# An AdaLN block of attention scan and FP4 feed-forward: the mix is turned by DMA as 16-bit planes, and the next group's work stands earlier in each engine's order

## What is computed

```python
h = _layernorm(x, axis=-1) * (1 + ca) + sa
x = x + ga * _L0_attn_ref(h, ...)      # RMS norm; q, kv, a = h @ W.T; a = sigmoid(a)
                                       # y[t] = a[t] * y[t-1] + kv[t];  returns q * y
h = _layernorm(x, axis=-1) * (1 + cb) + sb
x = x + gb * _L0_ffn_ref(h, ...)       # fp4_linear gate, up; silu(gate) * up; fp4_linear down
```

## Time and profile before

| | |
|---|---|
| median of 3 runs | 1963.17 us (1962.25 to 1963.4) |
| the profiled execution | 1961.58 us, of which the span of the trace is 1959.8 |
| mean granted TensorE clock | 0.998 |
| PE, DVE, ACT, POOL busy | 99%, 86%, 32%, 61% |
| DMA queue of SP | 45.1% of 16 engines' span |

### The profile page before, as it was taken

One profiled execution on the slowest core, in us unless ns is written; L12 is line 12 of the kernel. 1 busy time (PEld: TensorE's weight loads), 2 busy tenths in 40 slices (PEclk: granted clock), 3 DMA queues, 4 the chain that ended last, 5 costly groups with the idle time before them and its releaser, 6 DMA issues.

```text
span 1959.8 us, 27185 instructions
## 1 busy us (share of the span) xinstructions
PE 1936.3 (99%) x9403; PEld 927.2 (47%) x9403; DVE 1686.6 (86%) x2106; ACT 629.5 (32%) x885; POOL 1198.9 (61%) x1072
## 2 busy tenths in 40 slices
PE   8999999999999999999999999999999999999998
PEld 3444444444444444444444444444444444444444
DVE  7786767676868999999999999999999999999986
ACT  4333433343413233233233323323232332322221
POOL 1554764546535777677667667767766776776641
PEclk9999999999999999999999999999999999999999
DMA  8866665757552433433433343343334334333323
GB/s 292 272 178 144 174 170 149 174 142 200 125 129 69 108 74 80 98 75 72 92 89 72 81 100 74 74 94 88 73 84 96 72 76 97 80 72 87 88 62 77
DMA packets 421251, 218.22 MB, mean 111 GB/s; under 512 B 359858, under 2 KB 359870, under 8 KB 421188
## 3 DMA queue, kind: packets, MB, share of 16 engines
q1 hardware_dynamic: 421188, 217.39, 45.1%
HBM read 95.43 MB, written 33.57 MB: 66 GB/s over the span
## 4 chain that ended last, share of the span: by engine, by line
PE 87%; DVE 6%; issue 2%; POOL 2%; DMA 1%; ACT 1%; SPq 1%; DVEq 0%; POOLq 0%
PE bank L1067 43%; PE bank L986 20%; PE bank L1087 15%; PE bank L1091 7%; PE bank L1011 1%; SPq L398 1%; DVE arena L1163 1%; DMA arena<-arena 1%; DVE bn L1152 1%; DVE arena L1292 0%; DMA arena<-in_L_attn_x_dram 0%; DVE arena L1454 0%; PE bank L925 0%; DMA arena<-in_L_ffn_w_up_dram 0%; DVE arena L1461 0%
## 5 line engine op out<-in xcount | busy, mean ns | idle before, releaser
L1067 PE MATMUL bank<-wgu_hi,arena 128*128 128x512 f16 (+1 forms) x3072 | 869.9, 362 | 2.0 <-DVE arena L1401 2.0
L1067 PE MATMUL bank<-wgu_lo,arena 128*128 128x512 f16 (+1 forms) x1536 | 555.7, 362 | 0.0
L986 PE MATMUL bank<-arena,wq_hi 128*128 128x512 f16 x1536 | 458.5, 380 | 2.3 <-DMA arena<-arena 1.3
L1067 PEld LDWEIGHTS bank<-wgu_hi,arena 128*128 128x128 f16 x3072 | 300.5, 98 | 310.1 <-issue 2.4
L986 PE MATMUL bank<-arena,wq_lo 128*128 128x512 f16 x768 | 292.3, 381 | 0.0
L1087 PE MATMUL bank<-wd_hi,arena 128*128 128x512 f16 x693 | 263.0, 379 | 0.1
L1087 PE MATMUL bank<-wd_lo,arena 128*128 128x512 f16 x693 | 263.0, 380 | 0.0
L986 PEld LDWEIGHTS bank<-arena,wq_hi 128*128 128x128 f16 x1536 | 150.0, 98 | 178.4 <-issue 3.7
L1067 PEld LDWEIGHTS bank<-wgu_lo,arena 128*128 128x128 f16 x1536 | 150.2, 98 | 153.7
L663 POOL TENSOR_TENSOR arena<-arena 128x512 f32<-128x512 f32 x63 | 153.2, 2431 | 95.4 <-DVE arena L1476 95.4
L1401 DVE SCALAR_TENSOR_TENSOR arena<-bank,small,arena 128x512 f32<-128x512 f32 (+1 forms) x192 | 134.1, 701 | 85.8 <-PE bank L1067 81.5
(11 more groups left out here) (162 smaller groups left out, 2743.6 us busy)
## 6 DMA issues: line engine op xcount, KB each, us to landing
arena<-in_L_attn_x_dram SPq DMA_DIRECT2D x32, 1024.0 KB, 5.9
arena<-x_scratch SPq DMA_DIRECT2D x128, 256.0 KB, 3.2
x_scratch<-arena SPq DMA_DIRECT2D x16, 1024.0 KB, 4.4
out_dram<-arena SPq DMA_DIRECT2D x64, 256.0 KB, 3.1
arena<-in_L_wmod_dram SPq DMA_DIRECT2D x6, 1024.0 KB, 14.4
arena<-arena SPq DMA_TRANSPOSE x258, 3.5
wgu_hi<-in_L_ffn_w_gate_dram SPq DMA_DIRECT2D x1, 2816.0 KB, 12.3
wgu_lo<-in_L_ffn_w_up_dram SPq DMA_DIRECT2D x1, 2816.0 KB, 19.0
```

Of the source, the lines that this page charges most:

```text
L986: last = pe.matmul(dst[m % 2][:, :].rearrange("p (j t) -> p j t", j=NJ), w[:, k, at], uT[p][:, half, :, k, :], start=(n == 0), stop=(n == ...
L1067: last = pe.matmul(dst[n][:, 0:w], xT[p][:, half, k, :], wt[:, k, cut], start=(m == 0), stop=(m == 3 * KD - 1))
```

## The change

The 256 transposes of TensorE go, and with them `mixT`, `mix_turned` and TensorE's waits for them. In their place:

- `mix` writes its product over the decay buffer. It keeps the last column of each state in `carry` (a copy of 128x1), so two state buffers serve instead of four.
- `split_mix` (ScalarE, 4 in a group, 128x1024 16-bit elements): copies the float32 product as two planes of 16-bit words, low and high, into `mix_bits`. `decays` of the chunk two later waits for it.
- `turn_mix` (SP, 2 in a group): one transposing DMA for chunks 0 and 1, one for 2 and 3, each 2048 16-bit columns (16 blocks of 128).
- `join_mix` (ScalarE, 4 in a group, 128x1024 16-bit elements): puts the planes together again into one of two row buffers, from which `add_x` reads instead of from PSUM.

The order of work changes on four engines. In group i, ScalarE now does all `squares` and, behind the first two joins, `u_hi` ahead of the second chunk's decay; `apply(i + 2)` stands before the last decay. VectorE does the statistics and `u_lo` ahead of the second chunk's `mix`. SP turns the next u ahead of storing x1. In group 15 the second-half turn of group 14, the storing and the first-half turn of group 15 all stand ahead of `turn_x(0)`. The `add_x` of group 15 moves from the start of tile 0 to its end.

```diff
+        mix_bits = view(CH * GT).bitcast(U16).rearrange("p (q h j m t) -> p q h j m t", q=2, h=2, j=NJ, m=HC)
...
+        mixT_bits = view(NJ * D).bitcast(U16).rearrange("p (q h j c) -> p q h j c", q=2, h=2, j=NJ)
...
+        state = [view(GT) for _ in range(2)]
+        mix_rows = [view(D) for _ in range(2)]
...
+                def turn_mix(i, q):
+
+                    sp.wait_ge(mix_split, CH * i + HC * (q + 1))
+                    wait(sp, mix_joined, NJ * i)
+                    sp.nop(nofuse=True)
+                    sp.dma_start(mixT_bits[:, q].rearrange("p h j (m c) -> p (h j m) c", c=P),
+                                 mix_bits[:, q].rearrange("p h j m t -> p (h j m t)"),
+                                 transpose=True).then_inc(mixT_loaded[q], 16)
...
+                    if i:
+                        turn_mix(i - 1, 1)
+                    if i == NGA - 1:
                         for t in range(2):
                             load_normalised(t + 2, t)
+                    if i < NGA - 1:
+                        turn_u(i + 1, 1 - p)
                     weight_turns(i, -1, 0)
                     if i == 0:
-                        turn_u(1, 1)
                         load_group(3)
                         ffn_rows()
                         load_weights(0)
+                        turn_mix(0, 0)
                     else:
                         sp.wait_ge(x1_ready, NJ * i)
                         sp.dma_start(x1_group[i - 1], xr).then_inc(x1_stored, 16)
+                        turn_mix(i, 0)
+                        if i < NGA - 1:
+                            load_group(i + 3)
                         sp.wait_ge(x1_stored, 16 * i)
                     sp.dma_start(xr, x_group[i]).then_inc(xr_loaded, 16)
-                    if 0 < i < NGA - 1:
-                        turn_u(i + 1, 1 - p)
-                        load_group(i + 3)
                     weight_turns(i, 1, 3)
...
-                sp.wait_ge(x1_ready, NJ * NGA)
-                sp.dma_start(x1_group[NGA - 1], xr).then_inc(x1_stored, 16)
-                sp.wait_ge(x1_stored, 16 * NGA)
+                turn_mix(NGA - 1, 1)
                 for t in range(-1, 3):
                     slot(t, t % 2)
+                    if t == 0:
+                        sp.wait_ge(x1_ready, NJ * NGA)
+                        sp.dma_start(x1_group[NGA - 1], xr).then_inc(x1_stored, 16)
+                sp.wait_ge(x1_stored, 16 * NGA)
...
-                    wait(act, state_ready, CH * i + m - 1)
...
+                def split_mix(i, m):
+
+                    q = m // HC
+                    act.wait_ge(mix_ready, CH * i + m + 1)
+                    wait(act, mixT_loaded[q], 16 * i)
+                    act.activation(mix_bits[:, q, :, :, m % HC, :],
+                                   decay[m % 2].bitcast(U16).rearrange("p (j t h) -> p h j t", j=NJ, h=2),
+                                   ACT.Copy).then_inc(mix_split, 1)
+
+                def join_mix(i, js):
+
+                    for q in range(2):
+                        act.wait_ge(mixT_loaded[q], 16 * (i + 1))
+                    for j in js:
+                        wait(act, x1_ready, NJ * i + j - 1)
+                        act.activation(mix_rows[j % 2].bitcast(U16).rearrange("p (q c h) -> p q c h", q=2, h=2),
+                                       mixT_bits[:, :, :, j, :].rearrange("p q h c -> p q c h"),
+                                       ACT.Copy).then_inc(mix_joined, 1)
...
+                    split_mix(i - 1, 3)
                     decays(i, 0)
                     if not more:
-
+                        join_mix(i - 1, (0, 1))
                         ffn_apply(0, 0)
                         ffn_apply(1, 1)
-                    weights(0)
-                    if more:
-                        squares(i + 1, 1 - p, (0, 1))
-                    decays(i, 1)
-                    if more:
-                        squares(i + 1, 1 - p, (2, 3))
-                        u_hi(i + 1, 1 - p)
-                    else:
+                        decays(i, 1)
+                        split_mix(i, 0)
+                        weights(0)
+                        join_mix(i - 1, (2, 3))
                         steps_of_x(0, 0)
                         x_hi(0, 0)
+                        weights(1)
+                        decays(i, 2)
+                        split_mix(i, 1)
+                        weights(2)
+                        ffn_apply(2, 0)
+                        steps_of_x(1, 1)
+                        decays(i, 3)
+                        split_mix(i, 2)
+                        x_hi(1, 1)
+                        ffn_apply(3, 1)
+                        weights(3)
+                        return
+                    squares(i + 1, 1 - p)
+                    join_mix(i - 1, (0, 1))
+                    u_hi(i + 1, 1 - p)
+                    decays(i, 1)
+                    split_mix(i, 0)
+                    weights(0)
+                    join_mix(i - 1, (2, 3))
                     weights(1)
                     decays(i, 2)
-                    weights(2)
-                    if not more:
-                        ffn_apply(2, 0)
-                        steps_of_x(1, 1)
-                    decays(i, 3)
                     if i + 2 < NGA:
                         apply(i + 2, p)
-                    if not more:
-                        x_hi(1, 1)
-                        ffn_apply(3, 1)
+                    split_mix(i, 1)
+                    weights(2)
+                    decays(i, 3)
+                    split_mix(i, 2)
                     weights(3)
                 groups(group)
+                split_mix(NGA - 1, 3)
...
-                def turn_mix(i, p, js):
-                    for j in js:
-                        if j == 0:
-                            pe.wait_ge(mix_ready, CH * (i + 1))
-                        wait(pe, x1_ready, NJ * i + j - 1)
-                        for m in range(CH):
-                            last = pe.transpose(t_bank[j % 2][:, m * P:(m + 1) * P], mixT[p][:, m, j * P:(j + 1) * P],
-                                                ident[:, :])
-                        last.then_inc(mix_turned, 1)
...
-                    if i == 1:
-                        pe.wait_ge(mod_copied, NROW)
-                    turn_mix(i - 1, 1 - p, (0, 1))
                     product_a(i, p, 1)
                     product_kv(i, p, 1)
-                    turn_mix(i - 1, 1 - p, (2, 3))
...
-                        turn_mix(NGA - 1, 1, (0, 1))
+                        pe.wait_ge(mix_ready, CH * NGA)
                     if not (isinstance(i, int) and (i < 2 or i == LAST)):
                         down(i - 2, p)
                     gate_up(i, p, 1)
-                    if isinstance(i, int) and i == 0:
-                        turn_mix(NGA - 1, 1, (2, 3))
...
-                    dve.tensor_tensor_scan(state[m], decay[m % 2], kv_bank[m % 2][:, :],
-                                           0.0 if first else state[m][:, GT - 1:GT],
+                    if not first:
+                        dve.wait_ge(carry_ready, CH * (i - 1) + m + 1)
+                    dve.tensor_tensor_scan(state[m % 2], decay[m % 2], kv_bank[m % 2][:, :],
+                                           0.0 if first else carry[:, m:m + 1],
                                            ALU.mult, ALU.add).then_inc(state_ready, 1)
                     dve.wait_ge(state_ready, CH * i + m + 1)
+                    dve.tensor_copy(carry[:, m:m + 1], state[m % 2][:, GT - 1:GT]).then_inc(carry_ready, 1)
                     dve.wait_ge(q_ready, CH * i + m + 1)
-                    wait(dve, mix_turned, NJ * (i - 1))
-                    dve.scalar_tensor_tensor(mixT[p][:, m, :], q_bank[m % 2][:, :], ga[:, m, b:b + 1], state[m],
+                    dve.scalar_tensor_tensor(decay[m % 2], q_bank[m % 2][:, :], ga[:, m, b:b + 1], state[m % 2],
...
-                        dve.wait_ge(mix_turned, NJ * i + j + 1)
-                        dve.tensor_tensor(xr[:, j, :], t_bank[j % 2][:, :], xr[:, j, :], ALU.add).then_inc(x1_ready, 1)
+                        dve.wait_ge(mix_joined, NJ * i + j + 1)
+                        dve.tensor_tensor(xr[:, j, :], mix_rows[j % 2], xr[:, j, :], ALU.add).then_inc(x1_ready, 1)
...
+                        add_x(i - 1, (2, 3))
+                        mix(i, p, b, 1, first)
+                        quantise_x(0, 0)
+                        first_stats(2)
+                        x_lo(0, 0)
+                        weights(1)
+                        mix(i, p, b, 2, first)
+                        weights(2)
+                        quantise_x(1, 1)
+                        mix(i, p, b, 3, first)
+                        x_lo(1, 1)
+                        first_stats(3)
+                        weights(3)
+                        return
+                    if two_more:
+                        stats_mean_var(i + 2, p)
                     add_x(i - 1, (0, 1))
```

(26 more changed lines are left out.)

31 lines of the change are left out of this document (21 added, 10 removed).

## The result

| | before | after |
|---|---|---|
| median of the runs, us | 1963.3 (1962.3 to 1964.1, 4 runs) | 2040.1 (2039.1 to 2041.5, 4 runs) |
| profiled execution, span | 1959.8 | 2037.4 |
| ratio of after to before | | 1.0392, interval 1.0374 to 1.0410 |

The change costs 77 us. I had said 1945, with a range of 1933 to 1967. A group of the middle takes 34.7 to 34.9 us, which is the group time of rival 3's milder case (34.7), but its price, the 16 blocks as such, is not what makes it.

A forecast was written before the change was run, and what follows sets the result against it. TensorE, busy 99% of the span, was taken to bound the kernel. 1961.6 - 24.4 - 3 + 1.5 + 7.7 + 1.7 - 1 = 1944.1, plus 1.6 to the median: 1945.7, say 1945 us, range 1933 to 1967.

The forecast's parts named there:

- rival 3: SP and DMA engines: the two 16-block turns make the ring longer than the old group; slower, chance 0.17.
- rival 3's milder case: SP: half of the 16-block turns' extra pro-rata issue time gives 34.7 us a group, 1992 us in all.
- Removed, 24.4 us: TensorE, groups 1 to 14: 16 transposes fewer save 1.74 us a group, if each can run in 31.08 us.
- ScalarE's copies, 1.0: ScalarE: each split or join copy takes 1.0 us, bounds 0.7 and 2.1; ScalarE busy 21.7 of 31 us.
- SyncE: 1.5 issue, 4.5 landing: SP and DMA engines: each 16-block transposing DMA takes 1.5 us to issue and 4.5 to the landing.
- The ring, 30.4 to 32.4: Second-half landing through joins, add_x, store and SP's burst to the next landing: 30.4 to 32.4 us against 31.08; cost 1.5.
- Store to landing: The ring's part on SP, from the store of x1 to the next second-half landing: 19 to 21 us.
- from the landing to the store of x1: The ring's part through the joins and VectorE's work to the last add_x: 11.4 us.
- Early hitches, 3 us taken back: First stage: 8.3 us go in early hitches, of which 3 us (0 to 7) would come back.
- Hand-over, +7.7 and +1.7 of clock: Last group to tile 0: turned x lands later, +7.7 us; TensorE idles some 7 us, its slowed clock adds 1.7.

The follow-up runs named there:

- e14: The changed kernel with the weights' load early, their turns late, and SyncE's turns and loads spread in groups 1 to 14: 1988.8 us, ratio 1.013.
- h2: The kernel before, with groups 6 to 13 by DMA, weights' load early, their turns late, SyncE's DMAs spread: 1947.6 us, ratio 0.992.
- e12: The kernel before with only 4 of TensorE's 16 transposes a group left from group 1 on (stale data): 1957.2 us, ratio 0.997.
- e7: The changed kernel, in groups 5 to 14 with x1's store and the loads of x, xr and weights issued by ScalarE, not SyncE: 2040.0 us, ratio 1.040.
- e4: The kernel before with only the change's new order of work on SyncE, ScalarE and VectorE: 1977.4 us, ratio 1.008.
- h1: The kernel before, with groups 6 to 13 by DMA in the new order, weights' load early, their turns late: 1960.8 us, ratio 0.999.

## Why the prediction was wrong, point by point

1. *Removed, 24.4 us.* The price was right: 31.1 us a group in e14 and h2, 31.5 in groups 6 to 9 of e12 (1.31 less than 32.8 was expected). That it is gained in every group was not: e12 gained 5 us of 19.6. There VectorE's waits for the weights grew from 40.5 to 57.5 us and TensorE waits 8.5 us for u's turns; groups 10 to 14 took 32.0 to 34.9 us all the same, and groups 1 to 5 gained nothing (170.6 for 170.9).
2. *ScalarE's copies, 1.0.* Right: 1.05 and 1.16 us, 21 of 31 busy, and halving the joins moves the middle by nothing (321.0 for 320.7).

```profile
L787 ACT ACTIVATE arena<-arena 128x1024 uint16<-128x1024 uint16 x64 | 71.3, 1162 | 105.3 <-issue 94.2 <-DMA arena<-arena 11.1
L777 ACT ACTIVATE arena<-arena 128x1024 uint16<-128x1024 uint16 x64 | 67.1, 1049 | 40.7 <-DVE arena L1344 40.7
```

3. *SyncE: 1.5 issue, 4.5 landing.* Right for a turn alone (1.6 to 2.0 and 4.3 in h2), wrong behind the store, where the issue takes 4.8. Rival 3 put that price on the 16 blocks; e7 and h2 show that it is the company.
4. *The ring, 30.4 to 32.4.* This is the first step that failed, and not where SyncE is. Store to landing was to take 19 to 21 us and took 19.7 to 20.7 in four periods: the first half's turn has 4.8 us of issue in it, but it stands where SyncE had waited 4.4 us for the store. What was mis-sized is VectorE's part, from the landing to the store of x1: 11.4 in the sum, 14.2 to 15.0 measured. In the period shown the joins start at 367.49:

```profile
367.49 2.24 ACT L787 ACTIVATE arena<-arena 128x1024 uint16<-128x1024 uint16 x2 [8.18 <-issue]
```

   The second `mix` ends 9.5 us behind that, not 7.5. I had taken VectorE as ready when the joins are, and had not walked it from its first entry, the normalise, whose load is issued at the end of the same burst: of the 34.96 us from store to store 7.3 are issues, 8.4 the load and 19.2 VectorE. And the last two add_x take 3.0 us, not 1.3: I had said that VectorE reads x "from the same length as before", but it now reads both inputs from SBUF while GpSimd dequantises. No run changes that alone; h2 still has it, and its groups take 31.1.
   The second half was to land 7 to 9 us after a group's start; in after its joins start 14.9 us behind the last `mix` (317.51 to 332.41). Where the DMAs are spread they start 6.3 us behind it (405.89 to 412.19 in e14).
5. *Early hitches, 3 us taken back.* This is the second step that failed, and the larger one: the term had no walk behind it, and the 11.7 us that it and the transposes were to give became 32.3 of loss. The order alone costs 15 of them (e4): GpSimd comes to the next u only behind a tile of weights there, so whatever is put behind u waits with it. The 11.4 us of `turn_maximum` are `weight_max`, moved behind the joins.
6. *Hand-over, +7.7 and +1.7 of clock.* The wait for `xT_loaded` is 7.7 us, and the granted clock behind it is 0.50, the lower level:

```profile
655.15 0.58 PE L1113 MATMUL bank<-wgu_hi,arena 128*128 128x512 f16 x1 [7.75 <-DMA arena<-arena]
```

```profile
655.20:658.20 3.00, 3.00 (x8) 1.05 (x9) 0.00 (x0) 2.51 (x3) 1.92 (x4) 0.50 0.37 84
```

   That it is 7.7 to the tenth is luck. (Its place, 530 to 550 us, did not fit my own sum, which puts it near 563.) An 11.1 us wait for `mix(15, 1)` stands before it, and 4.4 us for tile 0's turned h behind it; I had put that `mix` at 24.7, 1.4 late. It is behind the joins, which ended their wait at 619.86, 14.4 us after `mix(14, 3)` and not 7.5, since the second half's turn stands behind the burst there too. And the turned x landed 10.2 us after the first half's turn was issued (644.78 to 655.01), where I had 8.3, with 2.7 for a megabyte that at the rate of the earlier trace rows is 5.0:

```profile
619.86 2.24 ACT L787 ACTIVATE arena<-arena 128x1024 uint16<-128x1024 uint16 x2 [11.98 <-issue]
637.33 1.03 PE L1046 MATMUL bank<-arena,wq_hi 128*128 128x512 f16 x2 [11.07 <-DVE arena L1344]
```

The chances: 0.17 for a ring longer than the old group was too low for a ring that I myself had within 0.4 to 2.4 us of it, with VectorE assumed ready and its add_x unchanged. No rival had the early groups lose.

Left open: how much of the ring is the slow add_x, and what the 12.5 us of groups 0 and 1 and the 18.9 of groups 2 to 5 consist of, part by part. The order's share is shown, the rest is only placed. Nor was a hand-over by DMA found that costs nothing.

## What to carry to other kernels

Walk every ring, from each engine's first entry in the stage, not only the one that the new wait opens; when one is shortened, look for the second before trusting the gain. What a turn by DMA costs here was set by its company: put it where the DMA engines idle, ahead of stores and big loads and not behind them, and give the big transfers the idle stretch. When an input moves from PSUM to SBUF, look at what GpSimd does beside the operation that reads it. Work that leaves a full engine is worth its price only in the groups where that engine is what bounds; take the cheap trial (leave out three quarters of it) before building the replacement.

## What the runs showed of the hardware

- A 16-block turn: 1.6 to 2.0 us of issue and 4.3 (once 5.4) to the landing with the DMA engines free, 4.8 and 6.7 behind a 1 MB store (after), 8.1 to 9.5 and 11.0 to 12.4 behind 2.5 to 2.7 MB of loads (h1); 13.7 to 16.9 to the landing beside a store and loads from another engine's queue (three turns of e7). A second queue did not help.
- An addition of 128x512 on VectorE with both inputs in SBUF, started while GpSimd multiplies 128x1024, took 2.42 us in place of about 0.68, and GpSimd's operation 2.3 in place of 1.9 (after); with one input in PSUM it stayed at 0.68 and 1.9 (e4).
- In h2 the DMA engines are 88 to 99% busy in the middle groups at 203 to 215 GB/s, and TensorE waits for nothing. In after they were 68 to 71% busy and it waited in nearly every group: the busy share did not tell which kernel waits, the place in the period did.
